# Token model on one core, last stage: which engines centre and scale the rows ahead of the rounding

## The reference

```python
h = h + _L0_ffn_ref(_layernorm(h, axis=-1), weight_int8, weight_scale, bias)

def _layernorm(x, axis=-1, eps=1e-05):
    return (x - mean) / sqrt(var + eps)

def _L0_ffn_ref(x, weight_int8, weight_scale, bias):
    x_scale = maximum(abs(x2).max() / 127.0, EPS)          # one scale for all tokens
    x_int8 = clip(round(x2 / x_scale), -128, 127)
    acc = x_int8 @ weight_int8.T
    return acc * x_scale * weight_scale.T + bias
```

## Time and profile before

| what | value |
|---|---|
| median of 3 runs | 1307.63 us (1302.93 to 1309.92) |
| profiled execution | 1309.22 us, its span 1307.3 us |
| TensorE matmul busy, whole span | 1156.5 us, 88% |
| VectorE busy | 1083.3 us, 83% |
| ScalarE busy | 791.4 us, 61% |
| GpSimd busy | 698.2 us, 53% |
| last stage, from its first instruction (L1717) | 1250.20 us to the end |

### The profile page before, as it was taken

One profiled execution on the slowest core, in us unless ns is written; L12 is line 12 of the kernel. 1 busy time (PEld: TensorE's weight loads), 2 busy tenths in 40 slices (PEclk: granted clock), 3 DMA queues, 4 the chain that ended last, 5 costly groups with the idle time before them and its releaser, 6 DMA issues. The chain is left out here.

```text
span 1307.3 us, 25029 instructions
## 1 busy us (share of the span) xinstructions
PE 1156.5 (88%) x7317; PEld 764.9 (59%) x7324; DVE 1083.3 (83%) x1963; ACT 791.4 (61%) x1275; POOL 698.2 (53%) x2062
## 2 busy tenths in 40 slices
PE   2991055899999999999999999999999999999956
PEld 1550022567676757676666667676767676757534
DVE  5997979978888888888888888898888887776177
ACT  4666637374848484848485756657574848452367
POOL 8882010657575857575757575757666574730000
PEclk9999997899999999999999999999999999998979
DMA  9999901010101010101010000000010101000025
GB/s 363 408 408 417 372 10 42 8 36 1 36 2 35 2 35 0 35 2 33 5 30 11 24 17 17 18 16 22 13 35 0 35 0 35 2 19 1 1 68 190
DMA packets 36993, 91.60 MB, mean 70 GB/s; under 512 B 10125, under 2 KB 21474, under 8 KB 32594
## 3 DMA queue, kind: packets, MB, share of 16 engines
q1 hardware_dynamic: 33298, 81.32, 17.9%
q0 software_dynamic: 3072, 8.39, 1.7%
q10 hardware_dynamic: 576, 1.31, 0.3%
HBM read 81.29 MB, written 9.70 MB: 70 GB/s over the span
## 5 line engine op out<-in xcount | busy, mean ns | idle before, releaser
L796 POOL TENSOR_TENSOR stp<-Gs,X 128x32 f32<-128x32 f32 x900 | 260.8, 290 | 254.5 <-ACT X L769 176.2
L798 POOL TENSOR_TENSOR Gs<-Gs,stp 128x32 f32<-128x32 f32 x900 | 257.9, 287 | 70.4
L1193 PE MATMUL bank<-w_fc,gl 128*128 128x256 f32 x1024 | 246.8, 385 | 0.8 <-ACT gl L1182 0.7
L1172 PE MATMUL bank<-mT,w_fc 128*128 128x512 f32 x512 | 236.7, 595 | 1.5 <-ACT mT L1152 1.5
L1193 PEld LDWEIGHTS bank<-w_fc,gl 128*128 128x128 f32 x1024 | 190.5, 191 | 59.9 <-issue 25.3
L646 PE MATMUL bank<-xT,w_in 128*128 128x512 f32 x448 | 208.7, 606 | 0.4 <-DVE uT L1085 0.3
L958 ACT ACTIVATE uT<-bank,cols 128x512 f32<-128x512 f32 x64 | 47.9, 774 | 216.6 <-DVE sz L1092 197.8
L1172 PEld LDWEIGHTS bank<-mT,w_fc 128*128 128x128 f32 x512 | 94.9, 190 | 85.5 <-issue 79.7
L972 DVE SCALAR_TENSOR_TENSOR uT<-bank,cols,uT 128x500 f32<-128x500 f32 (+1 forms) x192 | 133.4, 735 | 2.3
L646 PEld LDWEIGHTS bank<-xT,w_in 128*128 128x128 f32 x448 | 82.1, 192 | 84.7 <-issue 78.4
L346 DVE TENSOR_TENSOR peak<-ring,peak 128x1536 f32<-128x1536 f32 (+2 forms) x67 | 115.3, 1721 | 8.2 <-ACT ring L248 6.5
(11 more groups left out here) (211 smaller groups left out, 1879.4 us busy)
## 6 DMA issues: line engine op xcount, KB each, us to landing
ring<-in_table SPq DMA_DIRECT2D x31, 1536.0 KB, 19.9
d_rep<-d_rows SPq DMA_DIRECT2D x128, 64.0 KB, 2.0
out<-res SPq DMA_DIRECT2D x16, 512.0 KB, 2.9
b_rep<-bc_rows SPq DMA_DIRECT2D x128, 32.0 KB, 1.8
c_rep<-bc_rows SPq DMA_DIRECT2D x128, 32.0 KB, 1.8
w_fc<-in_w_fc SPq DMA_DIRECT2D x2, 1024.0 KB, 9.3
ring<-in_table SPq DMA_DIRECT2D x2, 768.0 KB, 5.3
w_in<-in_w_in ACTq DMA_DIRECT2D x1, 1088.0 KB, 5.1
```

Source lines behind the costliest of these rows:

```text
L796: pool.tensor_tensor(stp[:], Gs[:, t, ::-1, :], X2[:, t, :, :], ALU.mult).then_inc(rec.sem, 1)
L798: pool.tensor_tensor(Gs[:, t + 1, :, :], Gs[:, t, :, :], stp[:], ALU.add).then_inc(rec.sem, 1)
L1172: last = pe.matmul(pj[n % 4][:, :], w_fc1[:, k, n * P:(n + 1) * P], mT[:, k, :], start=(k == 0), stop=(k == KD - 1))
L1193: last = pe.matmul(sbk[j // 2][:, (j % 2) * D:(j % 2 + 1) * D], gl[n % LEAD][:, j * LEN:(j + 1) * LEN], w_fc2[:, n, :], start=False, stop= ...
```

## The change

Row 3 moves from ScalarE and row 2 from VectorE to GpSimd, which centres both with a subtraction and a multiplication (the form that VectorE uses) straight from `mu3` and `rs_q`. `off_q` is no longer needed and goes. GpSimd's 16 groups are written out without a loop. The second rounding waits for both of GpSimd's rows, the first one for both of VectorE's.

```diff
-            off_q = tmp("off_q", [P, SEQS])
-            DROWS = G - 1
+            DROWS = 2
...
-            centred = signal("centred", 1)
+            centred = signal("centred", G - DROWS)
...
-                def centre(g, b, i):
-                    if later(i):
-                        act.wait_ge(rounded.sem, rounded.at(g - 2))
-                    act.activation(f32q[b][:, G - 1, :], rows(g, G - 1), ACT.Identity,
-                                   bias=off_q[:, bass.ds(g * G + G - 1, 1)],
-                                   scale=rs_q[:, bass.ds(g * G + G - 1, 1)]).then_inc(centred.sem, 1)
...
-                act.wait_ge(xs_step, 5)
-                centre(0, 0, 0)
-                centre(1, 1, 0)
+                act.wait_ge(xs_step, 4)
                 take_T(0, 0, 0)
-                centre(2, 0, 1)
                 take_T(1, 1, 0)
                 scale(0, 0, 0)
-                centre(3, 1, 1)
...
                 with act.Fori(2, GROUPS // 2) as i:
-                    centre(i * 2, 0, i)
                     take_T(i * 2 - 1, 1, i)
                     scale(i * 2 - 2, 0, i)
-                    centre(i * 2 + 1, 1, i)
...
+            @block.gpsimd
+            def _(pool):
+                def centre(g, b, i):
+                    if later(i):
+                        pool.wait_ge(rounded.sem, rounded.at(g - 2))
+                    for j in range(DROWS, G):
+                        pool.tensor_scalar(f32q[b][:, j, :], h[:, (g * G + j) * D:(g * G + j + 1) * D], mu3[:, g * G + j:g * G + j + 1],
+                                           rs_q[:, g * G + j:g * G + j + 1], ALU.subtract, ALU.mult) \
+                            .then_inc(centred.sem, 1)
+
+                pool.wait_ge(xs_step, 3)
+                for g in range(GROUPS):
+                    centre(g, g % 2, g // 2)
...
-                dve.scalar_tensor_tensor(off_q[:], mu3[:], -1.0, rs_q[:], ALU.mult, ALU.mult).then_inc(xs_step, 1)
...
                     for n in range(2):
-                        dve.wait_ge(rq.sem, rq.at(g, min(DROWS, 2 * n + 2)))
                         if n:
                             dve.wait_ge(centred.sem, centred.at(g))
+                        else:
+                            dve.wait_ge(rq.sem, rq.at(g))
```

## The result

The changed kernel takes 1310.74 us in the median of 19 runs (1306.12 to 1312.84) against 1307.33 of the kernel before on the same chips: a ratio of 1.0026, 95% interval 1.0017 to 1.0036. (The ratio is of fast runs alone, so one run of the kernel before that took 1798.45 us is not in it.) So it is slower by 3.4 us (2.2 to 4.7), where 1305 and a gain of 3.0 were forecast. Ten more runs of the same kernel gave 1.0026 again (1.0013 to 1.0038).

A forecast was written before the change was run, and what follows sets the result against it. VectorE's 2.84 us step was taken to bound the last stage; steps -2.4 and ramp -0.6 gave -3.0 us: 1306.2 from the profiled run, 1304.6 from the median, rounded to 1305 (likeliest case 1302 to 1307.5, range 1300 to 1313).

The forecast's parts named there:

- What bounds the kernel: Last stage: VectorE sets the pace by its own instructions, 2.84 us a step, with no wait in it.
- VectorE's part: Last stage: one centred row less, -0.32, and an exposed wait, +0.12; step 2.64 us, gain 2.4 us over 12 steps.
- p: Time of one centred row on GpSimd, taken as 0.55 us; it may be 1.0 or more.
- the 1.03 us power: GpSimd instruction in the trace, 1.03 us for 4 elements: the operation can matter more than its size.
- The start: Ramp of the last stage: `whole` of group 1 ready 0.6 us earlier, and all behind it: -0.6 us.
- The bound of +0.8: Ramp's slow bound: at p = 1.0 GpSimd's rows are ready at 1256.5 us, the rounding after that.
- The steps: Steady part of the last stage: 12 steps of 2.64 instead of 2.84 us, -2.4 us, contention taken as 0.
- The 1027 us rows: Trace rows where VectorE's centred rows and GpSimd's 0.25 us instructions ran together unslowed; taken to show no contention.
- The first: Rival: GpSimd's rows block VectorE's centred rows and roundings; at p = 0.68 step 2.95, 1308.5 us; chance 0.20.
- The second: Rival: GpSimd row of 1.0 us or more that also blocks; at p = 1.0 step 3.59, 1317.4 us; chance 0.20.
- ScalarE's 0.49: `centre` off ScalarE's queue: 2.72 becomes 2.23 us a step, worth nothing by itself in the steady part.
- The term of 0 for the tail: Tail: the wait of 2.19 us for a slow store neither goes nor moves surely; 0, bounds -2.2 and +2.2.

The follow-up runs named there:

- Two-one-one: Against the kernel before: VectorE centres rows 0 and 1, ScalarE row 2, GpSimd row 3; 1304.86 us, ratio 0.9984; run again 1304.08 us, 0.9985.
- ScalarE's row alone: Against the changed kernel: only ScalarE's row goes to GpSimd, VectorE keeps its three; 1305.34 us, ratio 0.9998 to the kernel before.
- three experiments with short or single GpSimd rows: Changed kernel with GpSimd computing only 64 or 128 of 256 columns (1305.87 and 1306.32 us), and two-one-one (1304.86 us).

## Why the prediction was wrong, point by point

- **What bounds the kernel: right.** VectorE's 2.84 a step. Two-one-one shortened it and won, if only in part by it (the tail gave 1.1 to 1.2 us); ScalarE's row alone won nothing.
- **VectorE's part: right.** -0.32 and +0.12 (the rounding that waits for the last centred row) gave 2.64; three experiments with short or single GpSimd rows have 2.64. In two-one-one the second row starts at 1277.69 and the rounding at 1278.13: the 0.44 of the forecast.
- **GpSimd's row: the step that failed first.** p was taken at 0.55 us, since "an instruction with one tensor input lies between" a memset's 0.41 and two tensors' 0.68: it doesn't. The upper end was about right (two tensors 0.72; a copy, not in the forecast, 0.40), but the form used is outside them, 1.22 alone and 1.44 in the mean beside VectorE. The warning, the 1.03 us power, stood in the text and set only a rival. This is what the start was lost by; the steps needed the second failure, contention put at 0, as by the forecast's own bound a row without contention is free up to p = 1.25.
- **The start: wrong by 4.7 us**, +4.1 for -0.6. With p = 1.44 a round is GpSimd's 2.9. The bound of +0.8 was worked out for p = 1.0 and only to `whole` of group 1; but the first additions stand in VectorE's own queue behind rounds 0 to 3, so four of GpSimd's pairs count and not two: 11.44 us, from 1248.94 to 1260.38. Eight rows of 1.22 would be 9.8, so an estimated 2.1 us of the loss is the row's own length and 1.7 contention. The low clock added 0.6 in the first profile, where the additions then stood 0.59 us waiting for turn_back, and nothing in the second.
- **The steps: wrong by 3.0 us**, +0.6 for -2.4. Contention was put at 0. The 1027 us rows misled: there the GpSimd instructions were 0.25 us long and of another form (two tensors); the row of 1.22 us beside the same form of VectorE stretches VectorE's row from 404 to 560 ns and is stretched itself by 0.2, beside a rounding by 0.7. Whether the length or the form makes the difference was not tried. The form that never stood beside GpSimd in the trace, the rounding, costs GpSimd most.
- **The rivals.** The first had the contention, with rows too short (0.68 us) and 1308.5 us as its time. The second had the mechanism (a row of 1.0 us or more that also blocks), and not the price: 3.59 a step at p = 1.0, where 2.87 at 1.44 was measured. VectorE is not held for the whole length of GpSimd's instruction. The Trainium skill (SBUF — State Buffer, "Who interferes with whom", the single rule) has the loser blocked fully for the whole instruction, and names VectorE's tensor_scalar as a form that can contend, but not one with a single input from SBUF outside the faster modes; in these runs contention stands beside the centred rows and roundings and not beside the PSUM additions, which agrees, but a 1.22 us GpSimd row delayed a centred row by 0.17 and not by up to 1.2, which doesn't.
- **The rest: right.** ScalarE's 0.49 worth nothing, no store that newly holds the steps, TensorE not the bound, tail unchanged (12.43 us in the mean for 12.53). The term of 0 for the tail was partly luck: the same stretch took 11.4 us in five of the experiments' profiles.

## What to carry to other kernels

An operation that the trace has never shown on an engine need not cost what lies between two others: measure that form alone before work is moved to it, and beside the forms that will run with it. For a helper engine that works a fixed number of groups ahead, its share should fall mostly into the window in which the main engine doesn't contend (here the additions from PSUM, 1.2 us: shares of 1.22 and 1.58 us cost the step nothing, one of 2.87 cost 0.23; nothing between was tried). In the start, where nothing is ahead yet, it is waited for directly (9.76 us to the first additions with a share of some 1.7 us, 12.3 to 12.9 with 2.9). Removing work from the engine that sets the pace did pay, once what went in its place fitted.

## What the runs showed of the hardware that was not expected

- GpSimd's subtract-and-multiply with one f32 tensor and two per-partition operands: 0.37 us and 3.3 ns a column (128x256: 1.22; with constants 1.08; one operation 0.86 to 0.93). With two tensors and one operation 0.72, a copy 0.40.
- Side by side: with VectorE's centred rows 1.42 and 0.56 us (alone 1.22 and 0.40), with its roundings 1.96 and 0.61 (1.22 and 0.42), with additions from PSUM no change on either. Where both run on without a gap they settle in one period, 2.87 and 2.99 us, without a semaphore that holds them.
- TensorE's clock came back between 6.0 and 12.5 us behind `rs_q`, after 13.7, 17.1 or 20.5 us at the lower level, and its later return cost 0.9 us where all else was the same.
